# Reordering the steps of attention joins and of a self-attention core in a one-core, four-sample transformer kernel

## The reference

```python
for tag, kind in [("L1sa", "self"), ("L1ca", "cross"), ("L1mlp", "mlp"), ("L2sa", "self"),
                  ("L2ca", "cross"), ("L2mlp", "mlp"), ("L3ca", "cross")]:
    h = layernorm(x)                                  # gain and shift, or modulation by silu(cond)
    if kind == "mlp":
        y = gelu(h @ w1 + b1) @ w2 + b2
    else:
        src = h if kind == "self" else context        # L3: a normalised and modulated context
        q, k, v = h @ wq + bq, src @ wk + bk, src @ wv + bv
        p = softmax(q @ k.T / 4)                      # per head; L1ca has a mask
        y = (p @ v) @ wo + bo
    x = x + y + row                                   # row: a bias, partly from silu(cond)
```

## Time and profile before

| | |
|---|---|
| median of 3 runs | 4129.81 us (4107.52 to 4133.94) |
| profiled execution | 4114.12 us, of which the span from first to last instruction is 4112.1 us |
| PE matmul busy | 3667.3 us (89%) |
| ACT busy | 2362.4 us (57%) |
| DVE busy | 2214.7 us (54%) |
| POOL busy | 863.9 us (21%) |
| mean granted TensorE clock | 0.932 |

### The profile page before, as it was taken

How to read it: one execution, slowest core, us unless ns; L and a number is a source line. 1 busy time by engine, 2 the same in 40 slices (tenths; PEclk the granted TensorE clock), 3 DMA queues, 4 the chain that set the end, 5 groups by cost and what they waited for, 6 DMA issues and landing times.

```text
span 4112.1 us, 65758 instructions
## 1 busy us (share of the span) xinstructions
PE 3667.3 (89%) x20057; PEld 2149.5 (52%) x20057; DVE 2214.7 (54%) x3536; ACT 2362.4 (57%) x4094; POOL 863.9 (21%) x558
## 2 busy tenths in 40 slices
PE   7999998988898889989988889889988798899888
PEld 5777773346434743356336643464347433663366
DVE  3342436843684447643855468437844576448554
ACT  2333335764676456754776467646764567547654
POOL 3222231014102310034005110241023100340051
PEclk8999998989999999999999989999998999899989
DMA  3000101000000010000001100010000100000000
GB/s 127 31 1 31 31 24 48 2 27 33 10 2 12 32 42 1 17 32 21 1 2 32 38 15 2 27 42 1 2 12 32 42 2 17 32 21 2 2 32 22
DMA packets 70778, 92.73 MB, mean 23 GB/s; under 512 B 9227, under 2 KB 57934, under 8 KB 70350
## 3 DMA queue, kind: packets, MB, share of 16 engines
q1 hardware_dynamic: 40958, 63.40, 4.6%
q10 hardware_dynamic: 29520, 25.39, 2.0%
HBM read 77.96 MB, written 9.50 MB: 21 GB/s over the span
## 4 chain that ended last, share of the span: by engine, by line
issue 74%; POOL 15%; PE 9%; ACT 1%; DVE 1%; POOLq 0%; DMA 0%; SPq 0%; ACTq 0%; DVEq 0%
PE ps L632 8%; POOL hidl L1759 3%; POOL hidl L1794 3%; POOL x L1785 2%; POOL ql L1818 1%; POOL small L1719 1%; POOL hTl L1726 1%; POOL kl L1818 1%; POOL W2h L1809 1%; POOL W1h L1809 1%; PE ps L917 1%; DVE tok L1415 1%; POOL W2l L1811 0%; POOL W1l L1811 0%; ACT qs L1332 0%
## 5 line engine op out<-in xcount | busy, mean ns | idle before, releaser
L1364 ACT ACTIVATE probs<-ps 128x512 f32<-128x512 f32 (+1 forms) x2176 | 1216.3, 634 | 392.5 <-PE ps L632 384.2
L1681 DVE TENSOR_REDUCE mxh<-ps 128x2 f32<-128x1024 f32 x1024 | 1207.9, 1220 | 321.1 <-PE ps L632 319.4
L632 PE MATMUL ps<-probs,v 128*32 128x512 f32 (+1 forms) x4864 | 671.1, 625 | 1.4 <-ACT probs L1364 1.4
L632 PE MATMUL ps<-qs,ks 64*128 64x512 f32 x2048 | 548.2, 479 | 12.2 <-DVE mxh L1681 10.7
L632 PE MATMUL ps<-ks,qs 64*128 64x512 f32 x2048 | 428.6, 472 | 121.4 <-DVE mxh L1681 101.5
L632 PEld LDWEIGHTS ps<-qs,ks 64*128 64x128 f32 x2048 | 263.0, 190 | 514.6 <-ACT probs L1364 346.0
L1719 POOL TENSOR_TENSOR small<-small 128x4 f32<-128x4 f32 x66 | 68.2, 1034 | 2093.8 <-DVE small L1409 2093.8
L632 PEld LDWEIGHTS ps<-ks,qs 64*128 64x128 f32 x2048 | 200.3, 190 | 335.8 <-DVE mxh L1681 225.1
L1332 ACT ACTIVATE qs<-ps,cols 128x512 fp32r<-128x512 f32 x288 | 182.5, 691 | 120.2 <-PE ps L632 120.2
L632 PE MATMUL ps<-hT,slot 128*128 128x512 f32 x448 | 224.3, 632 | 28.8 <-ACT hT L1147 21.5
L632 PE MATMUL ps<-slot,hT 128*128 128x256 f32 x896 | 224.9, 400 | 9.5 <-ACT hT L1375 9.3
(11 more groups left out here) (219 smaller groups left out, 6259.8 us busy)
## 6 DMA issues: line engine op xcount, KB each, us to landing
slot<-in_L_w SPq DMA_DIRECT2D x8, 1024.0 KB, 6.9
slot<-in_L_fc_w SPq DMA_DIRECT2D x8, 1024.0 KB, 5.0
adw<-in_L_adaln_w SPq DMA_DIRECT2D x4, 1536.0 KB, 6.3
xin<-in_x ACTq DMA_DIRECT2D x5, 1024.0 KB, 5.7
x_after_block<-x ACTq DMA_DIRECT2D x20, 256.0 KB, 2.3
xin<-x_after_block ACTq DMA_DIRECT2D x5, 1024.0 KB, 5.4
ew<-in_L_e_w SPq DMA_DIRECT2D x6, 768.0 KB, 12.3
x<-in_x ACTq DMA_DIRECT2D x4, 1024.0 KB, 7.6
```

The source lines that it names most:

```text
L632: return pe.matmul(out, lhsT, rhs, start=start, stop=stop)
L1364: ins = act.activation(dst, src, ACT.Exp, scale=SCALE)
L1681: dve.tensor_reduce(mxh[:, z, t, j // 2, j % 2, :], ps[:, a:a + 2, :], AX.X, ALU.max, negate=True).then_inc(dve_done, M.add(dve_done, name))
```

## The change

Nothing is computed otherwise. The steps of PASS are put in another order, and some K steps have another form.

In a self module: the value steps 2 and 3 and the key stacks (c 1, n 1) leave the stretch before the first unit. V 2 comes behind the row, the key stacks go into unit 0, in the 128-row form, and V 3 into unit 1. The silu step of L1sa moves from the start of the pass to right before its row. One A fewer is done before unit 0, and the cadence of `more` shifts by one A, so that around a turn the list has

```diff
-                  + [("V", 1)] + halves("q", 1, 1) + [("V", 2)] + halves("k", 1, 1))
+                  + [("V", 1)] + halves("q", 1, 1))
+        later = [("K", "AA--", "k", 1, 1), ("K", "--AA", "k", 1, 1), ("V", 3)]
...
         more(first_slot + 1)
-        put(tag, ("V", 3))
+        put(tag, *[("scond",)] * (tag == "L1sa"), ("R",), ("add",))
         more(first_slot + 2)
-        put(tag, ("R",), ("add",))
-        lead = first_slot + 4
+        put(tag, ("V", 2))
+        lead = first_slot + 3
...
                 put(tag, *[("S",) + units[u] + (j,) for j in range(2, GH)])
-                more(lead + min(3 * (u + 1), 2 * (u + 1) + 4))
-            if u == end - 4:
+                put(tag, *(later[:2] if u == 0 else later[2:] if u == 1 else []))
+                more(lead + min(3 * u, 2 * u + 4) + 2)
+            if u == end - 5:
                 put(tag, *[("aT", 0, c) for c in range(KC)])
-            elif u in (end - 3, end - 2):
-                put(tag, ("o", u - end + 3))
-            elif u == end:
+            elif u in (end - 4, end - 3):
+                put(tag, ("o", u - end + 4))
+            elif u == end - 2:
                 put(follow, ("N", 0))
...
     def cross_lead(tag, before):
         first, then = projections("q", 0)
         if before:
+            put(tag, ("zero",), ("T", 0))
             put(before, ("OT", GROUPS - 1, NH - 1))
             put(tag, *projections("k", 0))
             put(before, *[("aT", NH - 1, c) for c in range(KC)])
+            put(tag, ("K", "dddd", "k", 0, 0), first)
+            put(before, ("o", 2))
+            put(tag, ("K", "aaaa", "k", 1, 0))
+            put(before, ("o", 3))
+            put(tag, ("N", 1), ("K", "aaaa", "q", 0, 0), then, ("R",))
         else:
+            put(tag, ("T", 0), *projections("k", 0), ("N", 1), first, ("K", "dddd", "k", 0, 0), then, ("T", 1), ("K", "aaaa", "q", 0, 0),
+                ("K", "adad", "k", 1, 0), ("P", "q", 0, 1), ("R",))
...
-        put(tag, *maxima[:2], ("R",), ("K", "AAAA", "q", 1, 0))
+        put(tag, *maxima[:4], ("K", "AAAA", "q", 1, 0))
         if before:
-            put(tag, ("N", 1), *maxima[2:4], ("T", 1))
+            put(tag, ("T", 1), *maxima[4:8], ("P", "q", 0, 1), *maxima[8:10], ("V", 0), ("P", "q", 1, 1))
         else:
-            put(tag, *maxima[2:4])
-        put(tag, *maxima[4:6], ("P", "q", 0, 1), *maxima[6:9], ("P", "q", 1, 1), *maxima[9:12], ("V", 0))
-        for i, k in enumerate(singles("q", 0, 1)):
-            put(tag, maxima[12 + i], k)
+            put(tag, *maxima[4:6], ("P", "q", 1, 1), *maxima[6:10], ("V", 0))
+        put(tag, *maxima[10:14], ("K", "aaaa", "q", 0, 1), *maxima[14:16])
         put(tag, ("add",), ("M", 0, 0))
...
-    put(MODULES[0][0], ("begin", 0), ("begin", 1), ("scond",), ("N", 0))
+    put(MODULES[0][0], ("begin", 0), ("begin", 1), ("N", 0))
```

More of the change, by code:

```diff
@@ L198, in self_attention @@
                 put(tag, *[("S",) + units[u] + (j,) for j in range(2, GH)])
-                more(lead + min(3 * (u + 1), 2 * (u + 1) + 4))
-            if u == end - 4:
+                put(tag, *(later[:2] if u == 0 else later[2:] if u == 1 else []))
+                more(lead + min(3 * u, 2 * u + 4) + 2)
+            if u == end - 5:
                 put(tag, *[("aT", 0, c) for c in range(KC)])
-            elif u in (end - 3, end - 2):
-                put(tag, ("o", u - end + 3))
-            elif u == end:
+            elif u in (end - 4, end - 3):
+                put(tag, ("o", u - end + 4))
+            elif u == end - 2:
                 put(follow, ("N", 0))
     def cross_lead(tag, before):
-        put(tag, *[("zero",)] * bool(before), ("T", 0))
+        first, then = projections("q", 0)
         if before:
+            put(tag, ("zero",), ("T", 0))
             put(before, ("OT", GROUPS - 1, NH - 1))
-        put(tag, *projections("k", 0))
-        if before:
+            put(tag, *projections("k", 0))
             put(before, *[("aT", NH - 1, c) for c in range(KC)])
-        else:
-            put(tag, ("N", 1))
-        put(tag, ("P", "q", 0, 0))
-        if before:
-            put(before, ("o", 2), ("o", 3))
-        put(tag, ("P", "q", 1, 0), *[("T", 1)] * (not before), ("K", "aaaa", "k", 0, 0), ("K", "AAAA", "q", 0, 0), ("K", "dddd", "k", 1, 0))
+            put(tag, ("K", "dddd", "k", 0, 0), first)
[3 more added lines that the diff above has]
+            put(tag, ("N", 1), ("K", "aaaa", "q", 0, 0), then, ("R",))
+        else:
+            put(tag, ("T", 0), *projections("k", 0), ("N", 1), first, ("K", "dddd", "k", 0, 0), then, ("T", 1), ("K", "aaaa", "q", 0, 0),
+                ("K", "adad", "k", 1, 0), ("P", "q", 0, 1), ("R",))
     def cross_attention(tag, follow, before):
```

## The result

The changed kernel takes 4198.1 us (median of 4 executions, 4197.7 to 4206.5), the kernel before in the same comparison 4130.0 (4107.5 to 4133.9): ratio 1.0181, 95% interval 1.0143 to 1.022. It is 68 us slower. The forecast was 4145 us and no change that can be told; the measured time lies above the forecast's own 4110 to 4175 and just inside the wider range of 4070 to 4200, four microseconds from the time of rival 1. Times in this document are medians without two far slower executions, of 5277 us (e10_before_cadence) and 7849 us (e16_turns_cross3).

What follows compares the result with a forecast made beforehand. PE, busy 3667 of 4112 us, was taken as the bound, in the core a DVE-PE chain. Terms 58 + 38 + 14 - 16 - 64 - 8 = +22 on 4114.1 gave 4136; median forecast 4145 us, range 4110 to 4175.

Steps and rivals of the forecast that it cites:

- rival 1: Self cores: the stalls cost the clock each time, +95 instead of +38 us; 4202 us, with fewer falls about 4185; chance 0.20.
- The turns, +58 and +38: Self cores: M waits 1.26 us for DVE's join at six turns, +58 us; two clock falls per core, +38 us.
- Rivals 2 and 3: Turns stall but the clock stays: 4097 us, chance 0.22; no stall, as M does not wait: 4049 us, chance 0.13.
- The cross leads, -43: L1ca and L2ca, T 0 to M: less idle, half clock and stack time, against new waits; -43 us.
- L3ca's lead, -8: L3ca's lead: -2 us per pass despite new waits and likely half clock; -8 us (-20 to +6).
- Start of the self core, +14: L1sa and L2sa: moved K and V 3 fill idle in units 0 and 1, even chances on the clock; +14 us.
- Start of a pass, -16: Pass start: without the silu step ACT evicts hT earlier, so the first P starts sooner; -16 us over four passes.
- Joins, -22: Joins of L1ca and L2ca: N 0 runs earlier, so T 0 comes 2.1 and 3.3 us earlier; -22 us.

Runs made afterwards that it cites:

- e10_before_cadence: Kernel before with the changed cadence alone (maxima one unit closer, turns placed for it; V 2, V 3, k(1,1) ahead of unit 0): 4136.9 us, ratio 1.0026.
- e16_turns_cross3: e15_tail_turns with the changed lead in L3ca added: 4065.9 us, ratio 0.9856 to the kernel before.
- e15_tail_turns: Kernel before with the changed tail, M (3,1) one unit behind its join and M (0,0) behind V 3: 4062.6 us, ratio 0.9849.
- e17_turns_cross3a: e16_turns_cross3 with all k(1,0) stacks of L3ca's lead on ACT: 4062.2 us, ratio 0.9844 to the kernel before.

## Why the prediction was wrong

The forecast of +22 us was +96 for the turns and -74 for everything else. Undone, the turns give 81 us. Everything else gave -9 us: 4117.1 us with the turns realigned, 4126.2 before, ratio 0.9986. So the loss came as forecast, and the gains that were to outweigh it did not. The sums of the two profiled executions over four passes show where (us):

| stretch | forecast | before | after, turns realigned | change |
|---|---|---|---|---|
| T 0 to M (0,1), L1sa and L2sa | +14 - 16 | 638.8 | 655.6 | +17 |
| M (0,1) to the next T 0, L1sa and L2sa | -22 | 1388.2 | 1365.5 | -23 |
| T 0 to M (0,1), L1ca and L2ca | -43 | 395.8 | 378.5 | -17 |
| T 0 to M (0,1), L3ca | -8 | 169.6 | 160.5 | -9 |
| M (0,1) of L3ca to the next T 0 | 0 | 115.2 | 125.1 | +10 |
| all else, with the expert block | 0 | 1404.5 | 1416.6 | +12 |

That is one execution of each, -10 us in sum, where the medians have -9; of the last row 10 us lie ahead of the first T 0, in the part that the change leaves alone. The gains fell short by 26 us in the leads of L1ca and L2ca and by 19 at the start of the self core and of the pass, and the restart cost 10.

**The turns, +58 and +38: right.** Forecast 1.26 us per turn and 24.9 us between M's; measured 1.17 and 24.8. Forecast two falls per core of about 6 us, 4.7 us lost; measured three of 3.4 us in L1sa's and two in L2sa's, at some 1.5 us each, 3.8 us per core. Undone, they give 81 us, against 96 for the two terms. Rival 1, a fall at each turn, did not occur, although its time (4202) is the one nearest to the result: it had the right sum from the wrong parts. Rivals 2 and 3 fall with the rows.

**The cross leads, -43: the step that failed.** Neither half of its sum held in full. In L1ca I forecast, per pass, 8.85 us less of PE's busy time (6.65 for the clock, 2.2 for the stacks) and 0.75 us more idle (3.1 for new waits, less 2.35). Measured are 5.4 us less busy time, as 6.8 us at half clock are left, and 2.4 us more idle (3.1 to 5.5). In L2ca the half clock all but went, 7 us in four leads instead of 50, and the busy time fell by 5.4 us; but the idle grew by 3.5 (3.9 to 7.4). The waits that I listed are there (0.71, 0.56, 1.20, 0.74). Those that I didn't are there too: aT 0.71 and the first K 0.92. So T 0 to M is 3.1 and 1.9 us shorter, of the 7.3 and 5.6 forecast.

M's 0.85 us I charged as idle alone, though I had just charged the clock for a like stall at the turns. It costs 3 us more behind two of L1ca's M's here, and behind all eight in L1ca and L2ca made alone. By themselves these two leads cost 38 us instead of saving 43, and there the half clock ahead of M did not go. That the one edit's price depends on the others is shown (42.9 us for L1ca's lead in the kernel with the leads alone, 36.3 in the one with all but the turns, on average); by which row isn't.

**L3ca's lead, -8: right.** The changed kernel has -9 in the stretch. The -10 us of its run alone is partly luck: there the stretch is 6 us shorter and the restart late.

**Start of the self core, +14: mis-sized.** The step that failed is that the moved K and V 3 fill idle time of PE in units 0 and 1. They stand between the bursts of A and leave DVE without maxima for 2.8 and 4.0 us, where it waits 0.6 and 0.9 without them, and the chain of maxima sets the second M. Without silu the start is 20 us longer in four passes and the kernel 26 us slower; with the same cadence and without the moved work it is as long as before. I had named that chain as the bound of the steady core, and at the start I gave it no price. Nor did the window of 13.6 us shrink: L1sa has 13.7 us at half clock around the first M and then twice 3.4.

**Start of a pass, -16: mis-sized.** P's wait shrank as forecast (0.94 us for under 1), and T 0 to P by 14 us in four passes. But nothing of it arrives at the second M: the time is that of before with silu alone moved, and T 0 to the second M is 341.4 us with silu and 341.6 without it in the kernels that have the new start. I had credited the time at P and not followed it to the row and to the maxima behind it. DVE's restart adds about 10 us of idle at the three starts, which no row of before shows. P's shorter wait gives part of it back.

**Joins, -22: right.** -21.4.

The single runs add up to 81 + 26 - 21 - 1 + 18 = 103 us, the change measured 68. So edits made together cost some 35 us less than apart, and half clock is where it shows. From 600 us on PE runs at half clock for 488 us before; the single edits would add 75 us to that, and the changed kernel has 475. Which gap kept the clock up is not told apart. Half clock alone doesn't order the kernels either: it is 406 us in one of 4062.6 us (e15_tail_turns) and 444 in one of 4062.2 (e17_turns_cross3a).

## What to carry to other kernels

A join whose result PE waits for must not have a long reduction queued ahead of it, and a list of steps that is aligned to a cadence has to be realigned when the cadence moves; one number here was worth 81 us. Where a matmul waits for a short step of another engine, look at what can stand ahead of it on PE: moving two matmuls' places (M (3,1) and M (0,0)) by one step each, with the tail, took 64 us off the kernel before. Cost a stretch by the chain that sets it, not by the idle time of the busiest engine. List every wait of a new order, not only those that have a like in the old one, and charge each new stall for the clock as well as for itself, or for neither. Sum a stretch over all passes of a trace: one pass of four can differ from the mean by 3 us and more.

## What the runs showed of the hardware

A stall of PE of 1.17 us was followed by a fall of the granted clock to 0.50 for 3.4 us behind every other turn in one kernel (20 falls in eight cores), and behind 14 of 48 turns in another with the same stall. One of 0.74 us, with a second of 0.6 behind it, was followed by 6.8 us at 0.50 in all eight cores of L1ca and L2ca in the kernel with their leads alone, in two of eight in the changed kernel, and never in L3ca. The Trainium skill ("TensorE: Matmul & The Clock Gate", A second HAM failure mode: psum-queue depth-cycling) says that short idles between groups of matmuls make the clock swing. The runs bear out the direction. The price was mostly the idle itself: the waits of the turns in the changed kernel are 53 us, of the 81 that came back without them.

DVE's restart at the start of a pass took 8.9 to 10.6 us in sum over three starts, or 18.4 to 19.4, without any wait in the profile, by an edit elsewhere in its program. The number of its instructions (1692 to 1700) and the number of packets fetched don't decide it: the kernel with 1700 and 123 packets restarts early, and so does that with 1692 and 119, while those with 1698 and 123 restart late.
